# Cross-attention and expert-choice FFN on one core: SBUF tiles placed at 128-byte multiples, three weight units split before the experts begin, gathered quarters turned one by one

## The chip, the cores and the metric

One NeuronCore of a Trainium2 chip runs the whole program. The metric is the device time of one execution in microseconds (us); a "run" is one execution timed from outside, and one execution was also recorded by the hardware profiler. PE is TensorE, DVE VectorE, ACT ScalarE, POOL GpSimd, SP the engine that issues most DMAs.

## The reference, cut to what matters

All in float32, with B=8 batches of S=224 queries, D=512, S2=750 context rows, 16 heads of 32, E=8 experts with I=2048:

```python
Q, K = rope(layernorm(x) @ Wq.T), rope(ctx @ Wk.T)
a = softmax(where(mask == 0, -inf, Q @ K.T / sqrt(32)))
x = x + tanh(g_xattn) * ((a @ (ctx @ Wv.T)) @ Wo.T)
y = layernorm(x)
gating, idx = top_k(transpose(softmax(y @ gate_w.T)), 56)
h = silu(y[idx] @ w_gate[e].T) * (y[idx] @ w_up[e].T)
x = x + tanh(g_ffn) * scatter_add(gating * (h @ w_down[e].T))
```

Each expert takes 56 rows of each batch, 448 rows in all.

## The kernel before, in words

A product that has to be exact to float32 is made of three matmuls in the type float32r: an operand w is split into w_hi (ACT copies it with rounding) and w_lo = w - w_hi (DVE subtracts), and PE adds w_hi x_hi, w_hi x_lo and w_lo x_hi in PSUM. The first operand of a matmul is the stationary one (loaded as weights), the second the moving one, which streams through PE one column at a time.

Three stages follow one another, each a block with barriers at its ends.

- `project_context`: for each batch, keys (L526 to L528, 24 matmuls of 376 moving columns for each of four groups; stationary `w_hi`/`w_lo`, moving `c_hi`/`c_lo`) and values (L537 to L539, 12 matmuls of 512 moving columns for each of six chunks k of 125 context rows; stationary `c_hi`/`c_lo` from row 125k on, moving `w_hi`/`w_lo`). That is 768 and 576 matmuls in the eight batches.
- `attend`: scores (L1282, moving `ks`), masking (L990), exp (L880), transposes (L1298), the product with the values (L1322, moving `e_t`), and between them the remainder of the batch before: projection out (L1222), second layer norm, gate logits, affinity. `every_batch` writes the order of every engine out by hand; `end()` of each engine is what is left after the last batch. There: residual (L1051), `moments` (L964, L967), POOL's `root` (L780, L782), `norm_2` (L975), transposes of xn2 (L1249), two copies into `xT` (ACT L857, DVE L1177), logits (L1262, L1061), affinity (L1063 to L1074), and seven top-8 rounds (L1080 to L1090). POOL's `end()` stores `xn_rows` (L810), adds the NaN flag into `x2o` (L795, two instructions) and stores `out` (L806), then waits for both stores. SP's `end()` loads the first four weight units into `w_raw` (L756), once the last score is made.
- `experts`: each of the 8 experts has 24 weight units of 128 x 1024: 16 for gate and up (`gate_up`, L1622 to L1624, 24 matmuls of 448 columns; moving `xs_hi`/`xs_lo`) and 8 for down (`down`, L1639 to L1641, 24 matmuls of 448 columns; moving `h_hi`, `h_lo`, `h_hi` in turn, one third of them `h_lo`). Units run through a ring of four slots; ACT (L1502) and DVE (L1552) split each unit three ahead (LEAD = 3). That is 3072 matmuls of the first kind and 1536 of the second. Before the first expert, gates and indices are turned onto the slot partitions (L1668), copied into `gate_t` (L1588) and `idx_t` (L1590), POOL copies one expert's indices into `gather_i` (L1469) and starts four indirect DMAs for the quarters of `xg` (L1472), PE turns all four (`turn_rows`, 16 transposes, L1608), and ACT (L1507) and DVE (L1557) split the turned rows into four pairs `xs_hi[:, c]`, `xs_lo[:, c]`. After the last expert there are transposes (L1650), scaling (L1562) and four scatters (L1482).

SBUF tiles are placed one behind another in the order of the code, each rounded up to 32 bytes, the first (`cst`) at byte 16512 of each partition. Worked out from that order, the starts modulo 128 are, before: `w_hi`, `w_lo` 0; `c_hi`, `c_lo` 32, with rows of 3008 bytes, so chunk c starts at 32 or 96 in turn; `ks`, `e_t`, `h_hi`, `ws_hi`, `ws_lo`, `xT`, `qs` 64; `sm`, `wo_sb`, `xs_hi`, `xs_lo`, `h_lo` 0. A key matmul's second half (columns 376 on) starts 1504 bytes later, which is 96 modulo 128; a value's chunk k starts 500k bytes later.

Of the kernel before, what the change touches and what calls it, by code (L numbers as in the profile page):

```python
# [10 lines left out]
U32 = mybir.dt.uint32  # L11
# [31 lines left out]
LEAD = 3  # L43
WAYS = 32
# [25 lines left out]
F_XT, F_Q, F_USES = 0, 2, 4  # L70

# [46 lines left out]
def program(nc, ctxT, x, maskq, wk, wv, wq, wo, gatew, gx, gf, wstream, consts, rotations, out):  # L118
# [5 lines left out]
    with ExitStack() as top:  # L124
# [15 lines left out]
        w_in = [sem(f"w_in{j}") for j in range(NRAW)]  # L140

        with ExitStack() as mid:
# [8 lines left out]
            with ExitStack() as late:  # L151
                sb(late, "below", [P, IC * SLOTS - E_OVER * (KC // 2) * PAIR])
                w_raw = [sb(late, f"w_raw{j}", [P, UNIT]) for j in range(NRAW)]
# [17 lines left out]

            project_context(nc, sem, sb, ps, both, ctxT, wk, wv, wq, x, maskq, gx, gf, consts, rotations, kd, vd, cst, gains)
            attend(nc, sem, sb, ps, both, x, maskq, wo, gatew, kd, vd, xn_rows, out, cst, ident,
                   cos, sin, gains, gate_all, row_all, wstream, w_raw, w_in)
        experts(nc, sem, sb, ps, w_raw, w_in, wstream, xn_rows, out_rows, cst, ident, gains, gate_all, row_all)


def project_context(nc, sem, sb, ps, both, ctxT, wk, wv, wq, x, maskq, gx, gf, consts, rotations, kd, vd, cst, gains):

    with ExitStack() as st:  # L180
        wraw, c_raw, k_split, v_out = both.wraw, both.c_raw, both.k_split, both.v_out
        w_hi = sb(st, "w_hi", [P, 2, DC, D], F32R)
# [422 lines left out]
def attend(nc, sem, sb, ps, both, x, maskq, wo, gatew, kd, vd, xn_rows, out, cst, ident,  # L605
           cos, sin, gains, gate_all, row_all, wstream, w_raw, w_in):

    with ExitStack() as st:
# [8 lines left out]
        sm = sb(st, "sm", [QP, SR, QC, SK])  # L617
        least, sums = sb(st, "least", [QP, KSLOTS, QC]), sb(st, "sums", [QP, 2, QC, HG])
        parts, spread = sb(st, "parts", [QP, 2, QC * HG]), sb(st, "spread", [QP, 2, QC, P])
        e_t = [sb(st, f"e_t{j}", [KP, KC // 2, PAIR]) for j in range(E_OVER, 2 * HG)] + both.e_t  # L620
# [65 lines left out]
        with nc.Block() as block:  # L686
            @block.sync
            def _(sp):
# [164 lines left out]
            def _(act):  # L853
# [95 lines left out]
            def _(dve):  # L949
# [143 lines left out]

                def start():
# [70 lines left out]
                def end():  # L1165
# [232 lines left out]
def experts(nc, sem, sb, ps, w_raw, w_in, wstream, xn_rows, out_rows, cst, ident, gains, gate_all, row_all):  # L1398

    with ExitStack() as st:  # L1400
        h_hi = sb(st, "h_hi", [P, IC, SLOTS], F32R)
        sb(st, "w_raw_place", [P, NRAW, UNIT])
        w_hi = [sb(st, f"ws_hi{j}", [P, UNIT], F32R) for j in range(NRAW)]
        w_lo = [sb(st, f"ws_lo{j}", [P, UNIT], F32R) for j in range(NRAW)]
        gate_t = sb(st, "gate_t", [RP, E, RG])
        idx_t = sb(st, "idx_t", [RP, E, RG], U32)
        gather_i, scatter_i = sb(st, "gather_i", [RP, RG], U32), sb(st, "scatter_i", [RP, RG], U32)
        xg = sb(st, "xg", [RP, RG, D])
        xs_hi, xs_lo = sb(st, "xs_hi", [P, DC, SLOTS], F32R), sb(st, "xs_lo", [P, DC, SLOTS], F32R)
        silu = [sb(st, f"silu{j}", [P, SLOTS]) for j in range(2)]  # L1410
        hid = [sb(st, f"hid{j}", [P, SLOTS]) for j in range(2)]
        h_lo = sb(st, "h_lo", [P, IC, SLOTS], F32R)
        y_cols = sb(st, "y_cols", [P, DC, SLOTS])
        y_sb = sb(st, "y_sb", [RP, RG, D])
# [5 lines left out]
        whi_done, wlo_done = sem("whi_done"), [sem(f"wlo_done{j}") for j in range(NRAW)]  # L1420
# [3 lines left out]
        gathered, x_turned, xhi_done, xlo_done = sem("gathered"), sem("x_turned"), sem("xhi_done"), sem("xlo_done")  # L1424
# [12 lines left out]
        with nc.Block() as block:  # L1437
            @block.sync
            def _(sp):
# [18 lines left out]
            def _(pool):  # L1458
# [5 lines left out]
                def gather(e):  # L1464


                    hold(x_turned, e)
                    hold(gathered, 16 * RG * e)
                    nc.gpsimd.tensor_copy(gather_i[:], idx_t[:, ds(e, 1), :].rearrange("p o g -> p (o g)")).then_inc(gidx_done, 1)  # L1469
                    hold(gidx_done, e + 1)  # L1470
                    for g in range(RG):
                        pool.indirect_dma_start(xg[:, g, :], None, xn_rows, bass.IndirectOffsetOnAxis(gather_i[:, g:g + 1], 0)).then_inc(gathered, 16)  # L1472

                def scatter(e):

                    hold(scattered, 16 * RG * e)
                    nc.gpsimd.tensor_copy(scatter_i[:], idx_t[:, ds(e, 1), :].rearrange("p o g -> p (o g)")).then_inc(sidx_done, 1)
# [7 lines left out]
                pool.wait_ge(idx_ready, 1)  # L1485
# [10 lines left out]
            def _(act):  # L1496
# [39 lines left out]

                for u in range(LEAD):
                    split_w(0, u)
# [199 lines left out]
```

## Time and profile before

| | us |
|---|---|
| median of 3 runs | 1840.67 |
| the three runs | 1840.67, 1841.35, 1837.13 |
| the profiled execution's own time | 1836.25 |
| its span, first to last instruction | 1834.4 |
| PE busy | 1740.8 (95%) |
| DVE / ACT / POOL busy | 1038.9 / 839.2 / 235.4 |

The span is shared out over the stages by the row of each stretch in the view by windows. A row of the timeline gives the start in us, the duration in us, engine, line, operation, tiles (written<-read), shapes and count. Matmul durations overlap, since PE works on several at once: what one costs in a stream is the distance from its start to the next one's start, called its pitch here.

### The profile page before, as it was taken

To read this page: it belongs to the slowest core of one execution; us is meant where nothing else is said; L and a number is where in the kernel's file an instruction comes from. 1 tells how busy PE (TensorE), PEld (TensorE's weight loads), DVE (VectorE), ACT (ScalarE), POOL (GpSimd) and SP (SyncE) were. 2 spreads that over 40 slices of the span, in tenths; PEclk is the share of its full clock that TensorE was granted. 3 is DMA by queue.
4 is the path that set the end of the run, shared out by engine and by line. 5 is a ranking of instruction groups with operands and counts; after the bars stand their busy time and mean duration, and the time that the engine had idled before them with its cause. 6 is when DMAs were issued, how large, how long until landed. Compare 5 with 4: busy or idle time off the path is not lost.

```text
span 1834.4 us, 28481 instructions
## 1 busy us (share of the span) xinstructions
PE 1740.8 (95%) x10502; PEld 1545.1 (84%) x10502; DVE 1038.9 (57%) x1786; ACT 839.2 (46%) x1482; POOL 235.4 (13%) x302
## 2 busy tenths in 40 slices
PE   7999999899999999983999999999999999999995
PEld 6898998677777877753999999999999999999995
DVE  6666667777887787754544535435445354453541
ACT  3223225777776877742433434424344243343430
POOL 0000002131231232122000102002020020010101
PEclk9999999999999999995999999999999999999998
DMA  6544547756755755523333535335343252353421
GB/s 242 224 173 186 189 156 220 182 126 153 178 147 135 183 150 134 141 87 96 115 104 103 150 109 143 103 103 151 106 121 127 106 149 104 101 150 109 124 92 20
DMA packets 76301, 251.90 MB, mean 137 GB/s; under 512 B 10784, under 2 KB 10784, under 8 KB 74928
## 3 DMA queue, kind: packets, MB, share of 16 engines
q1 hardware_dynamic: 64208, 216.55, 38.3%
q0 software_dynamic: 12000, 34.12, 7.9%
q8 instruction: 57, 0.93, 0.2%
q14 instruction: 36, 0.29, 0.1%
HBM read 188.01 MB, written 51.61 MB: 131 GB/s over the span
## 4 chain that ended last, share of the span: by engine, by line
PE 52%; POOL 1%; DVE 0%; issue 0%; DMA 0%; DVEq 0%; ACT 0%; POOLq 0%
PE gu_ps L1624 11%; PE gu_ps L1623 11%; PE gu_ps L1622 11%; PE y_ps L1641 6%; PE y_ps L1640 6%; PE y_ps L1639 6%; PE y_ps L1650 1%; PE gu_ps L1608 1%; POOL out L1482 0%; DMA xg<-xn_rows,gather_i 0%; POOL gather_i L1469 0%; POOL xg L1472 0%; DVE xs_lo L1557 0%; DVE y_cols L1584 0%; PE gu_ps L1668 0%
## 5 line engine op out<-in xcount | busy, mean ns | idle before, releaser
L1622 PE MATMUL gu_ps<-xs_hi,ws_hi 128*128 128x448 f32 x1024 | 370.3, 362 | 3.0 <-DVE xs_lo L1557 3.0
L1624 PE MATMUL gu_ps<-xs_hi,ws_lo 128*128 128x448 f32 x1024 | 371.9, 363 | 0.0
L1623 PE MATMUL gu_ps<-xs_lo,ws_hi 128*128 128x448 f32 x1024 | 371.8, 363 | 0.0
L1552 DVE TENSOR_TENSOR ws_lo<-w_raw,ws_hi 128x1024 fp32r<-128x1024 f32 x192 | 235.2, 1226 | 189.3 <-ACT ws_hi L1502 188.3
L1502 ACT ACTIVATE ws_hi<-w_raw 128x1024 fp32r<-128x1024 f32 x192 | 201.5, 1051 | 163.7 <-PE y_ps L1641 150.6
L1298 PEld LDWEIGHTS t_ps<-cst,sm 112*125 112x125 f32 x1536 | 205.0, 190 | 68.6 <-issue 29.3
L990 DVE CUSTOM_DVE_ANT_0 sm<-m_ps,mq 112x752 f32<-112x752 f32 x256 | 229.7, 935 | 34.2 <-PE m_ps L1282 33.8
L1298 PE MATMUL t_ps<-cst,sm 112*125 112x112 f32 x1536 | 233.3, 281 | 15.0 <-DVE e_t L998 11.3
L880 ACT ACTIVATE sm<-sm,least 112x752 f32<-112x752 f32 x256 | 234.7, 919 | 13.7 <-DVE least L990 12.7
L1622 PEld LDWEIGHTS gu_ps<-xs_hi,ws_hi 128*128 128x128 f32 x1024 | 192.0, 187 | 16.9 <-issue 3.3
L1623 PEld LDWEIGHTS gu_ps<-xs_lo,ws_hi 128*128 128x128 f32 x1024 | 192.7, 188 | 14.6
L1624 PEld LDWEIGHTS gu_ps<-xs_hi,ws_lo 128*128 128x128 f32 x1024 | 192.6, 188 | 10.4
L1523 ACT ACTIVATE silu<-gu_ps 128x448 f32<-128x448 f32 x128 | 69.8, 545 | 274.2 <-PE gu_ps L1624 272.2
L1641 PE MATMUL y_ps<-h_hi,ws_lo 128*128 128x448 f32 x512 | 187.8, 367 | 0.0
L1640 PE MATMUL y_ps<-h_lo,ws_hi 128*128 128x448 f32 x512 | 187.6, 367 | 0.0
L1639 PE MATMUL y_ps<-h_hi,ws_hi 128*128 128x448 f32 x512 | 187.4, 366 | 0.0
L887 ACT ACTIVATE e_t<-t_ps 125x448 f32<-125x448 f32 x256 | 137.4, 543 | 107.6 <-PE t_ps L1298 106.2
L1571 DVE TENSOR_TENSOR hid<-silu,gu_ps 128x448 f32<-128x448 f32 x128 | 79.6, 622 | 188.2 <-ACT silu L1523 188.2
L1482 POOL DMA_INDIRECT out<-y_sb,scatter_i x32 | 52.4, 1637 | 860.5 <-DVE y_sb L1562 853.2
L1574 DVE TENSOR_TENSOR h_lo<-hid,h_hi 128x448 fp32r<-128x448 f32 x128 | 80.0, 625 | 82.5 <-ACT h_hi L1525 81.8
L1282 PE MATMUL m_ps<-ks,qs 96*112 96x376 f32 x512 | 120.0, 355 | 5.0 <-PEq L227 1.7
L1525 ACT ACTIVATE h_hi<-hid 128x448 fp32r<-128x448 f32 x128 | 74.0, 578 | 88.0 <-DVE hid L1571 88.0
(153 smaller groups left out, 2438.6 us busy)
## 6 DMA issues: line engine op xcount, KB each, us to landing
w_raw<-wstream SPq DMA_DIRECT2D x192, 512.0 KB, 3.5
ks<-k_split SPq DMA_DIRECT2D x192, 188.0 KB, 5.4
k_split<-k_split SPq DMA_DIRECT2D x32, 752.0 KB, 3.4
v_rows<-v_out SPq DMA_DIRECT2D x16, 750.0 KB
vs<-v_rows SPq DMA_DIRECT2D x16, 750.0 KB
c_raw<-ctxT SPq DMA_DIRECT2D x7, 1500.0 KB, 13.0
qs<-q_hi POOLq DMA_DIRECT2D x64, 112.0 KB, 5.1
mq_raw<-maskq SPq DMA_DIRECT2D x7, 656.2 KB, 10.9
```

Source lines behind the costliest of these rows:

```text
L880: nc.scalar.activation(rows, rows, ACT.Exp, bias=least[:, h % KSLOTS, qc:qc + 1], scale=-1.0, accum_out=sums[:, h // HG % 2, qc, h % HG:h ...
L887: nc.scalar.activation(e_t[h % (2 * HG)][:, pc], t_ps[tile_of(b, h, pc) % 2][0:KP, 0:PAIR], ACT.Copy).then_inc(t_act, 1)
L990: nc.vector.tensor_tensor_reduce(sm[:, h % SR, qc].rearrange("p (a n) -> p a n", a=2), m_ps[qc][0:QP, :, 0:KN], mq[:, qc].rearrange("p (a ...
L1298: mm = nc.tensor.transpose(t_ps[n % 2][0:KP, a:a + QP], sm[:, h % SR, qc, c * KP:c * KP + KP], ident[0:QP, 0:QP])
L1502: nc.scalar.activation(w_hi[s][:], w_raw[s][:], ACT.Copy).then_inc(whi_done, 1)
L1552: nc.vector.tensor_tensor(w_lo[s][:], w_raw[s][:], w_hi[s][:], ALU.subtract).then_inc(wlo_done[s], 1)
L1622: nc.tensor.matmul(o, w_hi[s][:, w], xs_hi[:, c], start=(c == 0), stop=False)
L1623: nc.tensor.matmul(o, w_hi[s][:, w], xs_lo[:, c], start=False, stop=False)
L1624: mm = nc.tensor.matmul(o, w_lo[s][:, w], xs_hi[:, c], start=False, stop=(c == DC - 1))
L1639: nc.tensor.matmul(o, w_hi[s][:, w], h_hi[:, i], start=(i == 0), stop=False)
L1640: nc.tensor.matmul(o, w_hi[s][:, w], h_lo[:, i], start=False, stop=False)
L1641: mm = nc.tensor.matmul(o, w_lo[s][:, w], h_hi[:, i], start=False, stop=(i == IC - 1))
```

## The change

- Two pads of 64 bytes (`top_edge`, `mid_edge`), another order of the tiles, and rows of 768 instead of 752 elements in `c_hi`/`c_lo`. Worked out as above, all tiles named above now start at 0 modulo 128, and so does every chunk c of `c_hi` and `c_lo` (row 3072 bytes). Not moved to 0: the second half of a key matmul (now 96), a value's chunk k (500k), and the heads of `ks`, whose row stays 3008 bytes (0 or 64 by head, as before but the other way round).
- The tiles `ws_hi` and `ws_lo` exist from the last part of the attention on. ACT splits units 0 to 2 in the attention's `end()`, between `copy_parts` and `x2_columns`; DVE makes their low parts there too: unit 0 after `norm_2`, units 1 and 2 after its copy into `xT`, ahead of the logits.
- For expert 0, DVE writes `gather_i` straight from PSUM, ahead of `gate_t` and `idx_t`; POOL's copy is gone for that expert. SP holds its next weight loads until the four quarters of expert 0 have landed.
- Each quarter has its own semaphore; PE turns a quarter (four transposes) as soon as it has landed. The first unit's matmuls of chunk c wait only for `xs_lo[:, c]`.

```diff
+LINE = 32
+TOP_EDGE, MID_EDGE = 16, 16
+BEFORE = 2 * (B // 2) * D + DC * SLOTS + 2 * SLOTS
+FIRST = BEFORE + 3 * LINE
...
+        sb(top, "top_edge", [P, TOP_EDGE])
...
-                sb(late, "below", [P, IC * SLOTS - E_OVER * (KC // 2) * PAIR])
-                w_raw = [sb(late, f"w_raw{j}", [P, UNIT]) for j in range(NRAW)]
+                sb(late, "below", [P, FIRST - E_OVER * (KC // 2) * PAIR])
+                first = First(
+                    w_raw=[sb(late, f"w_raw{j}", [P, UNIT]) for j in range(NRAW)],
+                    w_hi=[sb(late, f"ws_hi{j}", [P, UNIT], F32R) for j in range(NRAW)],
+                    w_lo=[sb(late, f"ws_lo{j}", [P, UNIT], F32R) for j in range(NRAW)],
...
+            sb(mid, "mid_edge", [P, MID_EDGE])
...
+        c_hi = [sb(st, f"c_hi{j}", [P, DC, SK + LINE // 2], F32R) for j in range(2)]
+        c_lo = [sb(st, f"c_lo{j}", [P, DC, SK + LINE // 2], F32R) for j in range(2)]
...
                     copy_parts(B - 1, NG - 1)
+                    for u in range(LEAD):
+                        act.wait_ge(first.w_in[u], 16)
+                        nc.scalar.activation(first.w_hi[u][:], first.w_raw[u][:], ACT.Copy).then_inc(first.whi_done, 1)
                     x2_columns(B - 1, 0)
...
+                def low_w(u):
+                    dve.wait_ge(first.whi_done, u + 1)
+                    nc.vector.tensor_tensor(first.w_lo[u][:], first.w_raw[u][:], first.w_hi[u][:], ALU.subtract).then_inc(first.wlo_done[u], 1)
...
                     norm_2(b)
+                    low_w(0)
                     dve.wait_ge(rest_made, R_USES * b + R_XNT + 2)
                     nc.vector.tensor_copy(xT[:, 1], m_ps[1][:, 1, 0:2 * S]).then_inc(rest_free, 1)
+                    low_w(1)
+                    low_w(2)
                     logits(b)
...
+                for g in range(RG):
+                    hold(gathered[g], 16)
                 for u in range(NRAW, NU):
                     load(0, u)
...
-                    hold(x_turned, e)
-                    hold(gathered, 16 * RG * e)
-                    nc.gpsimd.tensor_copy(gather_i[:], idx_t[:, ds(e, 1), :].rearrange("p o g -> p (o g)")).then_inc(gidx_done, 1)
-                    hold(gidx_done, e + 1)
+                    if isinstance(e, int) and e == 0:
+                        hold(gidx_done, 1)
+                    else:
...
-                for u in range(LEAD):
-                    split_w(0, u)
                 split_x(0)
...
                 dve.wait_ge(turned, 1)
+                nc.vector.tensor_copy(gather_i, gu_ps[0][0:RP, RG * E:2 * RG * E].rearrange("p (g e) -> p g e", g=RG)[:, :, 0:1]
+                                      .rearrange("p g o -> p (g o)")).then_inc(gidx_done, 1)
...
-                    pe.wait_ge(gathered, 16 * RG * (e + 1))
-                    for c in range(DC):
-                        for g in range(RG):
+                    for g in range(RG):
+                        pe.wait_ge(gathered[g], 16 * (e + 1))
+                        for c in range(DC):
                             mm = nc.tensor.transpose(gu_ps[c][:, g * RP:g * RP + RP], xg[:, g, c * P:c * P + P], ident[0:RP, 0:RP])
...
-                    if u == 0:
-                        pe.wait_ge(xlo_done, DC * (e + 1))
...
                         for c in range(DC):
+                            if u == 0 and k == 0:
+                                pe.wait_ge(xlo_done, DC * e + c + 1)
```

## Rows read from the trace of the kernel before

**Rows 1.** View by windows: us, then busy us (count) per engine, PEclk, DMA
```profile
20.00:215.00 195.00, 195.00 (x984) 175.03 (x983) 130.86 (x175) 57.81 (x84) 0.96 (x2) 1.00 0.51 191
...
860.50:1834.00 973.50, 954.14 (x4848) 889.85 (x4848) 426.62 (x505) 358.67 (x505) 88.35 (x73) 0.99 0.37 114
```

**Rows 2.** Chain of waits, 841 to 861 us: start us, us, what
```profile
841.06 0.94 PE gu_ps L1668 x4
...
842.47 3.36 POOL gather_i L1469
...
846.71 1.05 POOL xg L1472
...
850.55 3.58 DMA xg<-xn_rows,gather_i
...
854.27 3.23 PE gu_ps L1608 x16
...
858.11 2.23 DVE xs_lo L1557 x4
...
860.47 0.71 PE gu_ps L1622
```

**Rows 3.** Timeline, DVE and POOL around the first two gathers
```profile
842.19 0.21 DVE L1590 CAST idx_t<-gu_ps 112x32 uint32<-112x32 f32 x1
842.28 3.48 DVE L1552 TENSOR_TENSOR ws_lo<-w_raw,ws_hi 128x1024 fp32r<-128x1024 f32 x3
...
857.69 0.18 POOL L1469 COPY gather_i<-idx_t 112x4 uint32<-112x4 uint32 x1 [6.21 <-PE gu_ps L1608]
...
858.64 0.95 POOL L1472 DMA_INDIRECT xg<-xn_rows,gather_i  x1 [0.77 <-POOL gather_i L1469]
```

**Rows 4.** Timeline of the attention's end, 809 to 828 us
```profile
809.02 1.86 SPq L756 DMA_DIRECT2D w_raw<-wstream  x4
...
820.71 1.00 DVE L975 TENSOR_SCALAR xn<-x_res,mv,rstd 112x512 f32<-112x512 f32 x2 [1.42 <-POOL rstd L782]
...
823.09 3.11 POOL L795 TENSOR_SCALAR x2o<-x_res,flags_sb 112x512 f32<-112x512 f32 x2
823.17 0.62 DVE L1177 COPY xT<-m_ps 128x448 f32<-128x448 f32 x1 [1.46 <-PE m_ps L1249]
...
827.04 0.17 DVE L1061 COPY lg<-w_ps 112x16 f32<-112x16 f32 x1 [3.25 <-PE w_ps L1262]
```

**Rows 5.** DMA issues (808 to 812 us; whole span): count, KB each, median us to landing
```profile
w_raw<-wstream SPq DMA_DIRECT2D x4, 512.0 KB, 7.2
...
out<-x2o POOLq DMA_DIRECT2D x8, 448.0 KB, 9.5
```

**Rows 6.** Timeline: matmuls of gate and up, 96 starts apart (units 4 to 7 of the second expert)
```profile
1000.44 0.36 PE L1622 MATMUL gu_ps<-xs_hi,ws_hi 128*128 128x448 f32 x1
...
1019.64 0.36 PE L1622 MATMUL gu_ps<-xs_hi,ws_hi 128*128 128x448 f32 x1
```

**Rows 7.** Timeline: matmuls of down, 120 starts apart (the first expert's last five units)
```profile
955.03 0.36 PE L1639 MATMUL y_ps<-h_hi,ws_hi 128*128 128x448 f32 x1
...
979.47 0.37 PE L1622 MATMUL gu_ps<-xs_hi,ws_hi 128*128 128x448 f32 x1
```

**Rows 8.** Timeline: keys (24), values of k=0 (12); then values of k=3 to 5 (36)
```profile
82.63 0.34 PE L526 MATMUL k_ps<-c_hi,w_hi 128*128 128x376 f32 x1
...
86.75 0.39 PE L537 MATMUL v_ps<-w_hi,c_hi 128*125 128x512 f32 x1
...
89.57 0.34 PE L526 MATMUL k_ps<-c_hi,w_hi 128*128 128x376 f32 x1
...
107.55 0.40 PE L537 MATMUL v_ps<-w_hi,c_hi 128*125 128x512 f32 x1
...
115.86 0.34 PE L526 MATMUL k_ps<-c_hi,w_hi 128*128 128x376 f32 x1
```

**Rows 9.** Timeline: ten float32 matmul records of 224 columns, moving `xT`
```profile
506.65 2.06 PE L1208 MATMUL w_ps<-xT,wq_sb 128*128 128x224 f32 x10
```

More of the change, by code:

```diff
@@ L70 @@
 F_XT, F_Q, F_USES = 0, 2, 4
+@dataclass
+class First:
+    w_raw: object
+    w_hi: object
+    w_lo: object
+    w_in: object
+    whi_done: object
+    wlo_done: object
 @dataclass
@@ L605, in attend @@
 def attend(nc, sem, sb, ps, both, x, maskq, wo, gatew, kd, vd, xn_rows, out, cst, ident,
-           cos, sin, gains, gate_all, row_all, wstream, w_raw, w_in):
+           cos, sin, gains, gate_all, row_all, wstream, first):
     with ExitStack() as st:
@@ L617, in attend @@
         sm = sb(st, "sm", [QP, SR, QC, SK])
+        e_t = [sb(st, f"e_t{j}", [KP, KC // 2, PAIR]) for j in range(E_OVER, 2 * HG)] + both.e_t
         least, sums = sb(st, "least", [QP, KSLOTS, QC]), sb(st, "sums", [QP, 2, QC, HG])
         parts, spread = sb(st, "parts", [QP, 2, QC * HG]), sb(st, "spread", [QP, 2, QC, P])
-        e_t = [sb(st, f"e_t{j}", [KP, KC // 2, PAIR]) for j in range(E_OVER, 2 * HG)] + both.e_t
         c_r, cx = sb(st, "c_r", [P, S]), sb(st, "cx", [P, NG, S])
@@ L1395, in _, with experts @@
                 every_batch(start, body, end)
-def experts(nc, sem, sb, ps, w_raw, w_in, wstream, xn_rows, out_rows, cst, ident, gains, gate_all, row_all):
+def experts(nc, sem, sb, ps, first, wstream, xn_rows, out_rows, cst, ident, gains, gate_all, row_all):
     with ExitStack() as st:
[L1401 to L1404, printed above, removed]
+        xg, y_sb = sb(st, "xg", [RP, RG, D]), sb(st, "y_sb", [RP, RG, D])
+        y_cols = sb(st, "y_cols", [P, DC, SLOTS])
+        silu = [sb(st, f"silu{j}", [P, SLOTS]) for j in range(2)]
         gate_t = sb(st, "gate_t", [RP, E, RG])
         idx_t = sb(st, "idx_t", [RP, E, RG], U32)
-        gather_i, scatter_i = sb(st, "gather_i", [RP, RG], U32), sb(st, "scatter_i", [RP, RG], U32)
-        xg = sb(st, "xg", [RP, RG, D])
+        both_i = sb(st, "both_i", [RP, LINE], U32)
+        gather_i, scatter_i = both_i[:, 0:RG], both_i[:, LINE // 2:LINE // 2 + RG]
+        sb(st, "first_place", [P, 3 * NRAW, UNIT])
+        w_raw, w_hi, w_lo = first.w_raw, first.w_hi, first.w_lo
         xs_hi, xs_lo = sb(st, "xs_hi", [P, DC, SLOTS], F32R), sb(st, "xs_lo", [P, DC, SLOTS], F32R)
-        silu = [sb(st, f"silu{j}", [P, SLOTS]) for j in range(2)]
         hid = [sb(st, f"hid{j}", [P, SLOTS]) for j in range(2)]
-        h_lo = sb(st, "h_lo", [P, IC, SLOTS], F32R)
-        y_cols = sb(st, "y_cols", [P, DC, SLOTS])
-        y_sb = sb(st, "y_sb", [RP, RG, D])
+        h_hi, h_lo = sb(st, "h_hi", [P, IC, SLOTS], F32R), sb(st, "h_lo", [P, IC, SLOTS], F32R)
         gu_ps = [ps(st, f"gu_ps{j}", [P, 512]) for j in range(4)]
         y_ps = [ps(st, f"y_ps{j}", [P, 512]) for j in range(RG)]
-        whi_done, wlo_done = sem("whi_done"), [sem(f"wlo_done{j}") for j in range(NRAW)]
+        w_in, whi_done, wlo_done = first.w_in, first.whi_done, first.wlo_done
         w_used = sem("w_used")
```

32 lines of the change are left out of this document (17 added, 15 removed).

## The prediction

> **What bounds the kernel now.** I read the view by windows first, to see which engine a stage waits for. In the projection of the context PE is busy for all 195 us of a 195 us stretch, and from 860.5 us to the end it is busy for 954 of 973 us [rows 1]. So in both stages a matmul's pitch is paid in full, and nothing that DVE, ACT or a DMA gains there counts. The page's 95% for PE hides the rest: between the attention and the experts PE hardly works, and there the chain of waits tells what is paid [rows 2]. It runs from the turning of the indices (PE, 841.06 us) over POOL's copy of them (3.36 us), the start of four gathers, the last one's landing (3.58 us after its issue at 850.55), 16 transposes (3.23 us), ACT's first split, and all four of DVE's, to the first expert matmul at 860.47. The timeline beside it shows why so small a copy takes so long: for the next expert the same copy of 112x4 takes 0.18 us, and here it runs beside DVE's three subtractions of weights, 842.28 to 845.76, and ends with them [rows 3].
>
> Then the pitch. 96 matmuls of gate and up take 19.20 us, 200.0 ns each [rows 6]; 120 of down take 24.44 us, 203.7 each [rows 7], at the same 448 columns. 200.0 ns is (448 + 32) columns at 2.4 GHz. By the layout, what differs is the moving tile: `xs_hi`, `xs_lo`, `h_lo` start at 0 modulo 128 and `h_hi`, which two of down's three matmuls stream, at 64.
>
> **The change part by part.** Its parts add up, as they lie in different stretches.
>
> (1) Indices. The gathers of expert 0 now start after DVE's small copy from PSUM. PE has turned the indices by 842.00 [rows 2]; the like conversion into `idx_t` takes 0.21 us [rows 3], so `gather_i` is there by 842.23. From the end of POOL's copy (845.83) to its first gather are 0.88 us [rows 2], for the next expert 0.77 [rows 3]; I take 0.85 and get 843.08 in place of 846.71, 3.6 us earlier. DVE's and ACT's weight splits leave this stretch altogether; they were on the path only by holding POOL's copy.
>
> (2) Quarters. The fourth issue follows the first by 3.84 us (850.55 - 846.71) and lands 3.58 us after itself: 850.50. That DMA path keeps its price: SP's next weight loads now wait until the quarters are in, which can only help, since before they ran beside the gathers. I leave it at 3.58; the upper bound is the same, the lower one issue distance less, 2.3, as if the quarter before had held it up by all of that. Issues stand 1.28 us apart (3.84/3), four transposes take 0.81 (3.23/4), so only the last quarter's are left when it lands: turned by 850.50 + 0.14 + 0.81 = 851.45, before 857.50. 6.05 us earlier, (1) included.
>
> (3) First matmul. It waits for one part of `xs_lo`, not four. The ACT step and its gaps keep 0.61 us (857.50 to 858.11), one DVE part is 2.23/4 = 0.56, and 0.13 to PE: 852.75 in place of 860.47, **7.7 us** in all. The parts behind it come every 0.56 us, while three matmuls take at least 0.60 [rows 6], so PE does not stall again. SP's held loads of units 4 to 6 are issued near 850.6; of four issued together the median took 7.2 us [rows 5], so the first is in well before 860, and PE wants unit 4 at 852.75 + 4 x 24 x 0.2 = 872 at the earliest. Hidden; if not, the ring of four would stall once.
>
> (4) Low and high parts at the attention's end. ACT waits there for weights that are issued from 809.0 to 810.9 [rows 4] and land 7.2 us later [rows 5], by 818.1. Its three splits, at most 1.16 us each (DVE's 3.48/3 [rows 3]; estimate), are over by 821.6. Behind them queues its copy into `xT`, for which the logits wait; DVE's half of it starts at 823.17 [rows 4], so they end in time. DVE's unit 0 (1.16 us) goes between 821.71 and 823.17, a hole of 1.46 us. Units 1 and 2 (2.32 us) go between 823.79 and 827.04, a hole of 3.25 us [rows 4]. So far the cost is nothing. But POOL adds its flag into `x2o` from 823.09 to 826.20, two instructions of 1.55 us [rows 4], and rows 3 show that a POOL instruction on SBUF and such a DVE subtraction exclude one another. Which of them waits is seen in rows 3 for POOL alone. If POOL waits, it is through at 828.5 in place of 826.20, and the `out` store behind it lands about 10 us later (9.5 in rows 5), by 838.7, before the experts' first instruction at 841.06 [rows 2], which waits for all of the attention: nothing; each us beyond 2.4 would be paid in full. If DVE waits, first for the rest of POOL's first instruction (to 824.65) and then for its second, unit 2 ends at 824.65 + 1.55 + 2.32 = 828.5, 1.5 us after the logits want DVE. I take **-0.5 us**, nearer the case of rows 3, with ends 0 and -1.6. The Trainium skill's page SBUF — State Buffer (Who interferes with whom) says that a DVE instruction with two SBUF inputs and a GpSimd one that reads SBUF share a port pair as a lock, held by whoever starts first. Rows 3 agree for POOL's side (3.35 us for 0.18); by that rule POOL, already running at 823.79, keeps DVE out here, which speaks against this place for units 1 and 2; by it the sum would be 1 us less, 12.6.
>
> (5) Down. `h_hi` moves from 64 to 0. If down then goes as gate and up do, 1536 x 3.67 ns = **5.6 us**. Bounds: 0, and a loss by the second rival.
>
> (6) Projection. Values of k=0 take (89.57 - 86.75)/12 = 235 ns, those of k=3 to 5 (115.86 - 107.55)/36 = 231 [rows 8]; (512 + 32) columns would be 226.7. Their moving tile was at 0 already, so here the stationary one costs. After the change only k=0 starts at 0: 96 x 8.3 ns = **0.8 us**; if every chunk profited, 0.8 + 480 x 4.1 ns = 2.8 us; if none, 0. Keys take (86.75 - 82.63)/24 = 171.7 ns [rows 8], with (376 + 32) columns at 170.0; half of their starts become 0, the other half stay off it. I take 0, with 768 x 1.7 ns = 1.3 us to either side.
>
> (7) The attention's streams. `ks` keeps its mix of offsets: 0. `e_t` goes from 64 to 0, but it is float32, and `xT`, float32 at 64, streams 224 columns in two beats at (2.06 - 0.36)/9 = 189 ns [rows 9], where 448 beats alone are 186.7: nothing to gain. Waits added on PE (three more per `turn_rows`, three in each expert's first unit) and POOL's four more holds per expert stand on things long done in experts 1 to 7: 0.
>
> Sum: 7.7 - 0.5 + 5.6 + 0.8 = **13.6 us**. The profiled execution took 1836.25 us (span 1834.4 and 1.85 around it), so its like would take 1822.6. It is the fastest of the four known; against the median of 1840.67 the sum gives 1827.1, and I forecast **1827**.
>
> **The rivals.**
> A. Placement does nothing. Down changes its PSUM bank every three matmuls, gate and up after twelve, and that could be the 3.7 ns. Against it: values stay twelve in one bank and still lie above their 226.7 [rows 8]. Left is 7.2 us: 1833.5.
> B. Slower. Offsets that are equal disturb one another: in down the moving `h_hi` and the stationary `ws_hi`, `ws_lo` both start at 64, in gate and up 0 meets 64. Then a matmul with equal offsets costs 3.67 x 3/2 = 5.5 ns more, and the change puts every pair of tiles at equal offsets: 3072 of gate and up and 512 with `h_lo`, 3584 x 5.5 = 19.7 us lost, against 7.2 won: 1853. It decides from 2.0 ns per matmul on. For it: keys, whose stationary tile is at 0, have the moving one at 0 in a quarter of them and are 1.7 ns off [rows 8]. Against it: values have moving 0 and stationary tiles at many offsets, none 0, and are worse than keys. The Trainium skill's page TensorE: Matmul & The Clock Gate (Part 2, What happens when you issue a matmul) gives the two operands independent read ports, which would leave B no ground; no row shows that.
> C. All of what a float32r matmul pays beyond its columns goes. Rows 9 show 448 beats in 189 ns. At that pitch 3072 x 11 + 1536 x 14.7 ns = 56 us go, with (1) to (4) 63: 1777. The same page of the Trainium skill (Back-to-back issue gap) has N/2.4 + 2.5 ns for a warm matmul by itself; the estimate from it is 189.2 here. Against it: `xs_hi`, `xs_lo` stream from 0 already and take 200.0.
> D. The hand-over is eaten: A holds, the lock of (4) costs its 1.6, and the gathers land no earlier because their path has a floor that rows 2 do not show; (2) and (3) keep 2.4 + 1.7 of their own. 2.5 us won, 1838.
>
> **How the numbers follow.** Forecast 0.72, A 0.12, B 0.08, C 0.03, D 0.05. A measurement of this kernel tells changes over 0.3% (5.5 us) from none. Faster: forecast, C and most of A, 0.86; same: D and a little of A, 0.06; slower: B, 0.08. Range: the low end is the profiled time less all upper ends, 7.7 + 1.3 (a landing in 2.3) + 5.6 + 2.8 + 1.3 = 18.7: 1817. The high end is A with the 1.6 of (4) and keys at their loss, 1840.67 - 7.7 + 1.6 + 1.3 = 1836. B, C and D, 0.16, are outside.
>
> **What would show it.** Right: no POOL copy before the first gather, which starts near 843; DVE's and ACT's splits of units 0 to 2 before 827; transposes in four groups; first expert matmul 12 us after the indices are turned (852.8 - 841.1), before 19.4; 120 matmuls of down in 24.0 us; 96 of gate and up still in 19.2; k=0 values at 227. Wrong: gate and up above 200.0 (B) or below (C), down at 203.7 (A), logits later than 5.3 us after `norm_2` (4), a wait of PE for `ws_lo` in units 1 to 4 (3).

## The result: 0.47% slower, against a forecast of 0.7% faster

| | before | after |
|---|---|---|
| median of 19 runs each, us | 1839.86 | 1848.73 |
| lowest to highest, us | 1837.13 to 1845.55 | 1842.68 to 1852.75 |
| span of the profiled execution, us | 1834.4 | 1844.1 |
| PE busy, us | 1740.8 | 1760.0 |
| index turning to first expert matmul, us | 841.06 to 860.47 | 840.97 to 853.85 |
| first expert matmul to the start of the last result transpose, us | 955.34 | 971.47 |
| from there to the end, us | 18.6 | 18.8 |

The ratio of the medians is 1.0047, with a 95% interval of 1.0039 to 1.0054: 8.6 us slower (7.2 to 9.9). The profile accounts for its own 9.7 us. The last index instruction of DVE starts at 840.46 us before and at 840.36 after, the first expert matmul comes 6.6 us earlier, the experts lose 16.1, and the tail 0.2.

View by windows of the kernel after, columns as in [rows 1]:

```profile
20.00:215.00 195.00, 195.00 (x981) 174.96 (x980) 130.84 (x174) 57.79 (x84) 0.96 (x2) 1.00 0.52 191
855.00:1844.00 989.00, 969.16 (x4846) 890.04 (x4845) 427.10 (x506) 359.15 (x506) 86.25 (x73) 0.99 0.38 113
```

Each stage still waits for PE alone: 969 us busy in 989, where [rows 1] have 954 in 973.5. DVE and ACT do the same work (427.1 and 359.2 us); PE's grew, and no engine or DMA stands in front of it.

Chain of waits of the kernel after, at the hand-over (start us, us, what), the answer to [rows 2]; `both_i` is the tile that now holds both `gather_i` and `scatter_i`:

```profile
840.97 0.94 PE gu_ps L1701 x4
...
841.93 0.17 DVE both_i L1621
...
842.14 0.85 issue
842.99 1.04 POOL xg L1508
...
845.59 5.07 DMA xg<-xn_rows,both_i
...
850.71 1.77 PE gu_ps L1641 x8
...
852.50 0.55 ACT xs_hi L1542
...
853.08 0.64 DVE xs_lo L1590
...
853.85 0.71 PE gu_ps L1655
```

POOL's copy is gone, and the first gather starts at 842.99, forecast 843.08. PE turns the quarters in groups, and one part of `xs_lo` is enough for the first matmul. One line is off: the chain goes over the third quarter, issued at 845.59 and 5.07 us on its way, not over the fourth with its 3.58 of before. PE's timeline shows it: a group for the first quarter, one for the second, and then eight transposes in a row: the third landed at 850.66, and the fourth, at 851.21, while the third was being turned.

```profile
846.45 0.98 PE L1641 MATMUL gu_ps<-cst,xg 112*128 112x112 f32 x4 [4.56 <-DMA xg<-xn_rows,both_i]
847.70 1.01 PE L1641 MATMUL gu_ps<-cst,xg 112*128 112x112 f32 x4 [0.26 <-DMA xg<-xn_rows,both_i]
850.71 1.76 PE L1641 MATMUL gu_ps<-cst,xg 112*128 112x112 f32 x8 [2.00 <-DMA xg<-xn_rows,both_i]
```

PE's timeline in the experts of the kernel after: 120 starts apart (down, first expert's last five units), 96 apart (gate and up, second expert, units 4 to 7), 96 apart (the same units, third expert):

```profile
950.14 0.36 PE L1672 MATMUL y_ps<-h_hi,ws_hi 128*128 128x448 f32 x1
...
974.46 0.36 PE L1655 MATMUL gu_ps<-xs_hi,ws_hi 128*128 128x448 f32 x1
...
995.85 0.37 PE L1655 MATMUL gu_ps<-xs_hi,ws_hi 128*128 128x448 f32 x1
...
1015.69 0.37 PE L1655 MATMUL gu_ps<-xs_hi,ws_hi 128*128 128x448 f32 x1
...
1117.97 0.37 PE L1655 MATMUL gu_ps<-xs_hi,ws_hi 128*128 128x448 f32 x1
...
1137.43 0.36 PE L1655 MATMUL gu_ps<-xs_hi,ws_hi 128*128 128x448 f32 x1
```

Here is the loss. (974.46 - 950.14)/120 = 202.7 ns for down, against 203.7 in [rows 7]; (1015.69 - 995.85)/96 = 206.7 ns for gate and up, against 200.0 in [rows 6]; (1137.43 - 1117.97)/96 = 202.7 in the next expert. Down follows its expert: its 120 starts from 1071.79 to 1096.59 in the second expert are 206.7 ns apart too. From the third unit of the first expert on, experts 0, 2, 4, 6 run at 202.7 and experts 1, 3, 5, 7 at 206.7, and the pitch changes only where the 16 transposes of a result stand in the stream. The mean is 204.7; before it was (2 x 200.0 + 203.7)/3 = 201.2. So 4608 x 3.4 = 15.8 us are lost. The duration that the profile prints for one matmul (0.36 or 0.37 us) hides this almost wholly: the distance of the starts is the cost.

The spans of two profiled executions also differ by up to some 12 us in the attention's first two batches (122.0 us before, 121.6 after, 121.0 to 133.1 in the experiments, 65.3 for every later batch in all of them); what is said below of times rests on the medians.

### The profile page after: what moved, and what is told of

Read it like the earlier page. It is cut to its first block, busy times and chain, and to the rows that moved or that the text cites. A ratio compares the mean times of both kernels' runs of the same rounds, so it can differ in the third digit from the quotient of the medians.

```text
span 1844.1 us, 28531 instructions
## 1 busy us (share of the span) xinstructions
PE 1760.0 (95%) x10502; PEld 1548.2 (84%) x10502; DVE 1039.3 (56%) x1787; ACT 839.6 (46%) x1482; POOL 230.6 (13%) x301
## 4 chain that ended last, share of the span: by engine, by line
PE 53%; POOL 0%; DMA 0%; issue 0%; DVE 0%; DVEq 0%; ACT 0%; POOLq 0%
PE gu_ps L1655 11%; PE gu_ps L1657 11%; PE gu_ps L1656 11%; PE y_ps L1672 6%; PE y_ps L1673 6%; PE y_ps L1674 6%; PE y_ps L1683 1%; PE gu_ps L1641 1%; POOL out L1518 0%; DMA xg<-xn_rows,both_i 0%; POOL xg L1508 0%; DVE y_cols L1617 0%; PE gu_ps L1701 0%; DVE y_sb L1595 0%; DVEq L1466 0%
## 5 line engine op out<-in xcount | busy, mean ns | idle before, releaser
L1655 PE MATMUL gu_ps<-xs_hi,ws_hi 128*128 128x448 f32 x1024 | 377.0, 368 | 1.4 <-DVE xs_lo L1590 1.4
L1657 PE MATMUL gu_ps<-xs_hi,ws_lo 128*128 128x448 f32 x1024 | 376.2, 367 | 0.0
L1656 PE MATMUL gu_ps<-xs_lo,ws_hi 128*128 128x448 f32 x1024 | 376.1, 367 | 0.0
L1655 PEld LDWEIGHTS gu_ps<-xs_hi,ws_hi 128*128 128x128 f32 x1024 | 192.9, 188 | 18.8 <-issue 1.7
L1518 POOL DMA_INDIRECT out<-y_sb,both_i x32 | 53.2, 1663 | 877.2 <-DVE y_sb L1595 869.9
L1313 PE MATMUL m_ps<-ks,qs 96*112 96x376 f32 x512 | 121.0, 358 | 3.2 <-PEq L247 1.7
```

Source lines behind the costliest of these rows:

```text
L1655: nc.tensor.matmul(o, w_hi[s][:, w], xs_hi[:, c], start=(c == 0), stop=False)
L1656: nc.tensor.matmul(o, w_hi[s][:, w], xs_lo[:, c], start=False, stop=False)
L1657: mm = nc.tensor.matmul(o, w_lo[s][:, w], xs_hi[:, c], start=False, stop=(c == DC - 1))
```

## The experiments

What counts turned out to be the start of a tile modulo 256, not 128. Modulo 256 the kernels stand so, with d = (start of the stationary tile - start of the moving one) modulo 256:

| | `ws` | `xs` | `h_hi` | `h_lo` | d in gate, up | d in down |
|---|---|---|---|---|---|---|
| before | 192 | 0 | 192 | 0 | 192 | 0, 192, 0 |
| after | 128 | 128 | 128 | 128 | 0 | 0 |

**1 to 4: the after kernel with pads.** All four keep the new order of work; only the starts in the experts change. They take these edits, in elements of four bytes, with the kernels that have each in brackets:

```diff
+SPLIT_EDGE = 16      # between w_raw and ws_hi, in attention and experts: ws 192 (1, 2, 4)
+        sb(st, "x_edge", [P, 16])     # before xs_hi (1, 2, 3)
+        sb(st, "hh_edge", [P, 16])    # before h_hi (1)
+        sb(st, "hl_edge", [P, 16])    # before h_lo (1)
```

Starts modulo 256 of `ws`, `xs`, `h_hi`, `h_lo`: the first 192, 0, 64, 128; the second 192, 0, 0, 0; the third 128, 192, 192, 192; the fourth 192 throughout. So d is 192 in gate and up of the first and 128, 64, 128 in its down, 192 everywhere in the second and third, and 0 everywhere in the fourth.

> The changed kernel with only the experts' tiles put back to the old offsets modulo 128: stationary ws_hi/ws_lo at 64, xs_hi/xs_lo at 0, h_hi at 64, h_lo at 0. T1 (what counts is how a matmul's stationary and moving starts lie to one another; equal is dear, 64 apart is free) and T2 (what counts is each tile's own offset, stationary at 0 being dear): gate and up back at 200.0 ns per matmul, down at 203.7, and some 6 to 7 us below the kernel before, 1833, which is what the earlier hand-over is worth. T3 (placement is innocent; the pitch went up by something else in the new schedule, such as the waits per chunk or where the splits run): gate and up stay at 203 to 207, about 1848.

> The changed kernel with the stationary tiles ws_hi/ws_lo alone moved to 64 modulo 128, all moving tiles of the experts left at 0. T1: all 4608 expert matmuls at 200.0 ns, 5.6 us below e1, about 1827. T2: the same 200.0 in gate and up and in down. T3: as the changed kernel, 203 to 207 ns. If down stays at 203.7 with h_hi at 0, its extra came from its bank change (rival A of the prediction).

> The changed kernel with ws_hi/ws_lo left at 0 and all moving tiles of the experts (xs_hi, xs_lo, h_hi, h_lo) at 64. T1: 64 apart again, so 200.0 ns in all, about 1827. T2: stationary at 0 is what is dear, so 203 to 207 ns, about 1848 or above. T3: as the changed kernel.

> The changed kernel with stationary and moving tiles of the experts all at 64 modulo 128. T1: equal offsets, so the 202.7 and 206.7 ns of the changed kernel, about 1848. T2: stationary off 0, so at or near 200.0, with at most what h_hi at 64 cost before, about 1827 to 1833. T3: as the changed kernel.

Measured, beside 21 runs of before (median 1839.26):

| | median, us (runs) | ratio to before, 95% | gate, up, ns | down, ns | start of the last index instruction to first expert matmul, us |
|---|---|---|---|---|---|
| 1, old mix | 1836.19 (11) | 0.9979, 0.9970 to 0.9988 | 200.0 | 204.4 | 12.2 |
| 2, `ws` 192, moving 0, d = 192 | 1830.29 (5) | 0.9948, 0.9934 to 0.9961 | 200.0 | 200.0 | 13.6 |
| 3, `ws` 128, moving 192, d = 192 | 1829.11 (4) | 0.9946, 0.9925 to 0.9966 | 200.0 | 200.0 | 13.5 |
| 4, all at 192, d = 0 | 1842.07 (10) | 1.0009, 0.9996 to 1.0021 | 202.7 | 202.7, in the first expert 206.7 | 13.4 |

PE's timeline in down's last five units of the first expert, 120 starts apart, in the second kernel:

```profile
960.12 0.36 PE L1678 MATMUL y_ps<-h_hi,ws_hi 128*128 128x448 f32 x1
...
984.12 0.36 PE L1661 MATMUL gu_ps<-xs_hi,ws_hi 128*128 128x448 f32 x1
```

The same in the fourth:

```profile
955.41 0.37 PE L1677 MATMUL y_ps<-h_hi,ws_hi 128*128 128x448 f32 x1
...
980.21 0.37 PE L1660 MATMUL gu_ps<-xs_hi,ws_hi 128*128 128x448 f32 x1
```

24.00 us against 24.80 for the same 120 matmuls on the same data. The fourth has the two pitches of after at other absolute starts, so neither 0 nor 64 modulo 128 is a bad place in itself; against the fourth the second shifts the moving tiles alone and the third the stationary ones alone, and both reach 200.0 everywhere. It is the pair that counts. The stretch shown of the fourth is its dear one: 206.7 holds for 8 of its 192 units, from the 16 transposes of gathered rows in the first expert (at 948.9 us) to the transposes of that expert's result, and all else runs at 202.7. That is why it stands at 1842 and not at the 1848 that was expected. And the new hand-over by itself wins: the first kernel is 3.9 us faster than before although its down is 1536 x 0.8 = 1.2 us dearer. Its expectation, 1833 us and 203.7 ns in down, was off because its starts repeat those of before modulo 128 only.

**5: a scan of starts.** A kernel of matmuls alone; it leaves out the whole reference and copies x to the output. Bursts of 48 float32r matmuls with a stationary load each, twelve to a bank as in gate and up, with 1, 4 and 3 transposes ahead of the bursts:

```python
nc.tensor.matmul(u_ps[k][:, 0:n], wt[:, s // 4 + (q // 3 % 8) * P:s // 4 + (q // 3 % 8) * P + P],
                 mt[:, m // 4 + c * 448:m // 4 + c * 448 + n], start=(q % 12 == 0), stop=(q % 12 == 11))
```

> A kernel of matmuls alone: float32r, 128x128 stationary and 448 moving columns (some pairs 376 or 512), three bursts of 48 for each pair of starts (stationary s, moving m, in bytes modulo 256), one to four float32 transposes between bursts. It computes nothing of the reference; x is copied to the output. T1: the pitch follows (s - m) modulo 128 alone: 200.0 ns at 64, 202.7 or 206.7 at 0 whatever m is, s = 128 or 192 like 0 or 64, and 32 and 96 somewhere between. T2 (own offsets): (0,64) and (64,64) differ from what T1 says. If 32 and 96 also give 200.0, only equal starts collide. 376 columns: 170.0 at 64 apart and 172 to 174 at equal starts. 512: 226.7 at 64 apart and up to 235 at 0.

With (s, m) the two starts and 448 columns it gave 202.7 ns at (0, 0), 202.2 at (64, 0), 203.8 at (128, 0) and 200.0 at (192, 0), 200.0 at (0, 64), but 202.2 at (128, 64), and 206.7 at (64, 64). So (64, 0) and (192, 0), the same modulo 128, are not the same: the rule in its form modulo 128, in which 64 apart was free either way, fell. A difference of 192 modulo 256, the stationary start 64 bytes below the moving one, is what was free each time; (32, 96) is the third such pair.

**6: before with `h_hi` and `h_lo` exchanged.** `h_lo`, one third of down, now starts at 192 and `h_hi`, two thirds, at 0; nothing else of before is touched.

```diff
-        h_hi = sb(st, "h_hi", [P, IC, SLOTS], F32R)
+        h_lo = sb(st, "h_lo", [P, IC, SLOTS], F32R)
...
-        h_lo = sb(st, "h_lo", [P, IC, SLOTS], F32R)
+        h_hi = sb(st, "h_hi", [P, IC, SLOTS], F32R)
```

> The kernel before with the places of h_hi and h_lo exchanged: h_hi, streamed by two of down's three matmuls, now starts at 0 modulo 128 and h_lo at 64, where ws_hi and ws_lo start. T1: the equal starts fall from two in three to one in three, so down goes from 203.7 to about 201.8 ns, 2.8 us in all, 1836.5, gate and up stay at 200.0. Rival A of the prediction (down's bank change): down stays at 203.7 and the time at 1839.3.

1837.54 us (10 runs) against 1839.44 (19), ratio 0.9986, 0.9977 to 0.9996. The same 120 starts as in [rows 7]:

```profile
955.04 0.37 PE L1639 MATMUL y_ps<-h_hi,ws_hi 128*128 128x448 f32 x1
...
979.30 0.37 PE L1622 MATMUL gu_ps<-xs_hi,ws_hi 128*128 128x448 f32 x1
```

202.2 ns, where [rows 7] give 203.7, with the same change of bank every three matmuls. The expectation had 201.8 ns. 202.2 is (2 x 200.0 + 206.7)/3, one third at the disturbed pitch of 206.7; but the same sum does not give the 203.7 of before (204.5 with two thirds at 206.7, 201.8 with two thirds at 202.7), nor do the scan's pitches give the 204.4 of kernel 1 (203.3). In a stream that mixes distances the pitches of unmixed streams don't add up, and no scan mixed them. The prediction's rival A, placement does nothing, falls.

**7: the second kernel with the three splits back at the experts' start.** ACT's and DVE's splits of units 0 to 2 leave the attention's end; the rest is kernel 2.

```diff
-                    for u in range(LEAD):
-                        act.wait_ge(first.w_in[u], 16)
-                        nc.scalar.activation(first.w_hi[u][:], first.w_raw[u][:], ACT.Copy).then_inc(first.whi_done, 1)
...
-                    low_w(0)
...
-                    low_w(1)
-                    low_w(2)
...
+                for u in range(LEAD):
+                    split_w(0, u)
```

> e2 with the splits of units 0 to 2 put back where they were, at the experts' start; DVE still writes gather_i from PSUM first, and the quarters are still turned as they land. If POOL's copy was all that the splits held up, the first expert matmul still comes 13.4 us after the last index is made (20.0 before), within 0.5, and the time is e2's, 1830. If DVE's subtractions also hold up POOL while it issues gathers, the first gather or its followers come up to 3.4 us later, so about 16.5 us and 1833.

POOL's timeline of this kernel at the gathers:

```profile
847.14 3.67 POOL L1508 DMA_INDIRECT xg<-xn_rows,both_i  x1 [15.24 <-DVE both_i L1623]
851.12 0.95 POOL L1508 DMA_INDIRECT xg<-xn_rows,both_i  x1 [0.30 <-issue]
852.37 0.93 POOL L1508 DMA_INDIRECT xg<-xn_rows,both_i  x1 [0.30 <-issue]
```

DVE's timeline beside it:

```profile
846.41 3.49 DVE L1587 TENSOR_TENSOR ws_lo<-w_raw,ws_hi 128x1024 fp32r<-128x1024 f32 x3
```

The first gather's issue, 1.04 us in the kernel after, takes 3.67 and is over 0.91 us after DVE's three subtractions; the others take their usual 0.95. ACT's three splits beside it run from 845.10 to 848.05 and end 2.8 us before that issue does, so they are not what it waits for. So it is not only a POOL copy that such subtractions hold: they hold the issue of an indirect DMA too. The first expert matmul comes 15.9 us after the start of the last index instruction, 13.6 in kernel 2. The median, 1830.15 us (10 runs, ratio 0.9950, 0.9935 to 0.9964), does not tell these 2.3 us from nothing: the interval is +-2.7 us wide.

**8: the scan again, modulo 256, with one to six transposes ahead of each burst of 36.** The edit is the list of starts and lengths and `enumerate((1, 2, 3, 4, 5, 6))`; it too leaves out the reference and copies x to the output.

> The kernel of matmuls alone again, six bursts of 36 for each pair of starts, after one to six transposes. R1: for 448 columns (s - m) modulo 256 decides, and 192 alone is free: (192,0), (64,128), (128,192) at 200.0 ns in every burst; (192,128), (0,192) differ by 64 and stand at 202.2; (0,0) and (64,64) change between 202.7 and 206.7 with the number of transposes before the burst, since both states hold once entered. R2: modulo 128 as first thought, then (192,128) and (0,192) are at 200.0 too. 512 columns: e5 had 226.7 at equal starts and 230 to 233 at 20 to 116; if the rule moves with the length, another difference than 192 is free, and (64,64), (128,128) are as (0,0). 376: one free difference near 192 at 170.4, the others 172 to 174.

PE's timeline of this kernel, one row a burst of 36 matmuls; the first two have both starts at 0, the next four both at 64, the last two have 192 and 0:

```profile
34.11 7.54 PE L69 MATMUL u_ps<-mt,wt 128*128 128x448 f32 x36
...
41.85 7.55 PE L69 MATMUL u_ps<-mt,wt 128*128 128x448 f32 x36
...
65.06 7.67 PE L69 MATMUL u_ps<-mt,wt 128*128 128x448 f32 x36
...
72.70 7.54 PE L69 MATMUL u_ps<-mt,wt 128*128 128x448 f32 x36
...
80.32 7.67 PE L69 MATMUL u_ps<-mt,wt 128*128 128x448 f32 x36
...
88.19 7.55 PE L69 MATMUL u_ps<-mt,wt 128*128 128x448 f32 x36
...
111.52 7.46 PE L69 MATMUL u_ps<-mt,wt 128*128 128x448 f32 x36
...
118.95 7.45 PE L69 MATMUL u_ps<-mt,wt 128*128 128x448 f32 x36
```

A burst is 35 pitches and 0.45 us for its two ends: 7.54 is a pitch of 202.7, 7.67 one of 206.7, 7.46 one of 200.0. With both starts at 64 the two alternate from burst to burst; with both at 0, against the expectation, every burst from the second on has 202.7. So the stream falls into one of two patterns and keeps it. The experts of the kernel after do the same, with 16 transposes between them. What picks the pattern is not shown: the number of transposes grows with each burst here, so it can't be told from the mere order, and in scan 5, with 1, 4 and 3 of them, (64, 64) stood at 206.7 all three times. All pairs of scans 5 and 8 with starts at multiples of 32, by d:

| d | 448 columns, ns | 512 columns | 376 columns |
|---|---|---|---|
| 0 | 202.7 or 206.7 | 226.7 to 227.9 | 173.3 |
| 32 | 204.4, once 203.3 | 233.3 | 173.3 |
| 64 | 202.2 | 233.3 | 170.0 to 173.3 |
| 96 | 200.0 or 206.7 | 234.4 | 171.7 |
| 128 | 203.8 | 232.6 to 233.3 | 173.3 |
| 160 | 205.3 | 233.3 | 173.3 |
| 192 | 200.0 (five pairs, every burst) | 228.9 | 170.4 |
| 224 | 200.0 to 206.7 | 233.3 | 173.3 |

The lowest value of each column is the column count + 32 at 2.4 GHz: 200.0, 226.7, 170.0. Which d gives it goes by the length: 192 for 448, 0 for 512. At 448 columns 192 gave 200.0 in every burst; it was expected to be the only one, but 96 gave it too, in seven bursts of nine. 376 columns reach 170.0 in one burst only, at 64; 384 columns reach their 173.3 at 192 in every burst and at 0 in two of six. Starts off this grid of 32 don't fit the table: (16, 16) has 200.3, (80, 16) has 206.7 and (0, 16) 200.0. So the distance alone is the rule only for starts at multiples of 32, as all tiles of the experts have them.

**9: the third kernel with `c_hi` and `c_lo` moved too**, for the projection's sake (their start goes from 128 to 192, that of `w_hi`, `w_lo` is 128):

```diff
+        sb(st, "c_edge", [P, LINE // 2])
         c_hi = [sb(st, f"c_hi{j}", [P, DC, SK + LINE // 2], F32R) for j in range(2)]
```

> e3 (stationary weights at 128 modulo 256, moving tiles of the experts at 192) with c_hi and c_lo also moved by 64: in the first half of the keys the stationary w_hi is then at 128 and the moving c_hi at 192, the difference of e3. R1: those 384 matmuls go from 173.3 to 170.4 ns, 1.1 us; values change by what their own table gives (between -2 and +2 us); the experts stay at 200.0. Time as e3 within 2 us, 1828.

1828.12 us (5 runs) against 1839.00 (15), ratio 0.9935, 0.9921 to 0.9950: the fastest of all, 12.0 us below before by its ratio, though its interval overlaps that of kernel 3. Keys of the first half go from 173.1 to 170.4 ns, those of the second from 173.2 to 172.1, and values stand at 232.7 to 234.8.

**10: kernel 2 with `x_edge` at 48 elements instead of 16**, so the moving tiles start at 128 modulo 256. That is 64 bytes apart as in kernel 2, but the other way round: d = 64.

```diff
-        sb(st, "x_edge", [P, 16])
+        sb(st, "x_edge", [P, 48])
```

> e2 with the experts' moving tiles 128 bytes further on: stationary at 192 modulo 256, moving at 128, so still at 64 and 0 modulo 128. R1 (modulo 256): the difference is now 64 and not 192, so 202.2 ns in all 4608 matmuls, 10 us above e2, 1840. R2 (modulo 128): 200.0 ns and e2's time, 1830.

Gate and up of the second expert, 96 starts apart:

```profile
993.87 0.37 PE L1661 MATMUL gu_ps<-xs_hi,ws_hi 128*128 128x448 f32 x1
...
1013.29 0.37 PE L1661 MATMUL gu_ps<-xs_hi,ws_hi 128*128 128x448 f32 x1
```

202.3 ns, and 24.26 us for down's 120, 202.2: the scan's value for d = 64, in all of the experts. 1838.75 us (10 runs), ratio 0.9994, 0.9982 to 1.0007. So a scan of bare matmuls gave beforehand what the placement costs in the full kernel, sign included.

**All of it together.** Let the hand-over win 5.9 us (6.6, less 0.7 below) and take each kernel's pitches from its own timeline:

| | hand-over | experts, us | sum against before | measured, 95% |
|---|---|---|---|---|
| after | -5.9 | 4608 x 3.4 = +15.8 | +9.9 | +8.6, 7.2 to 9.9 |
| 1 | -5.9 | 1536 x 0.8 = +1.2 | -4.7 | -3.9, -5.5 to -2.2 |
| 2 | -5.9 | -1536 x 3.7 = -5.6 | -11.5 | -9.6, -12.1 to -7.2 |
| 3 | -5.9 | -1536 x 3.7 = -5.6 | -11.5 | -9.9, -13.8 to -6.3 |
| 4 | -5.9 | 4608 x 1.6 = +7.4 | +1.5 | +1.7, -0.7 to +3.9 |
| 6 | 0 | -1536 x 1.5 = -2.3 | -2.3 | -2.6, -4.2 to -0.7 |
| 7 | -5.9 + 2.3 | -5.6 | -9.2 | -9.2, -12.0 to -6.6 |
| 9 | -5.9 | -1536 x 3.7 = -5.6 | -11.5 | -12.0, -14.5 to -9.2 |
| 10 | -5.9 | 3072 x 2.2 - 1536 x 1.5 = +4.5 | -1.4 | -1.1, -3.3 to +1.3 |

Measured is what the ratio makes of the median of before. Every sum lies in its interval, that of after at its very edge, and nothing is fitted: the hand-over is that of the kernel after throughout (with 2.3 more in kernel 7), the pitches are each kernel's own, and the projection is left out. The hand-over that kernel 1's one profile shows is 1.3 us shorter than that of after; taken into the sum it would make it -6.0, just outside. (For kernel 4: 202.7 in 184 units and 206.7 in 8 is a mean of 202.8, before 201.2.)

## Why the prediction was wrong, step by step

(1) **Indices: right.** First gather at 842.99, forecast 843.08; DVE's copy takes 0.17 us for 0.21.

(2) **Quarters: 1.1 us too early.** The last turning was forecast to end at 851.45 and ended at 852.47. The transposes' time held; the landing did not. 15 of the third quarter's 16 parts were in by 848.77, the last at 850.66, and the fourth quarter landed 4.38 us after its issue. Kernels 2, 3, 4, 7 and 9 show a like delay: their third quarter takes 4.9 to 5.2 us from its issue. Kernel 1 had none, 3.3 us, and so 12.2 us from the start of the last index instruction to the first matmul, which is the forecast's 852.75 - 840.5. I had kept 3.58 us as the price of the DMA path, from one profile. The cause is not shown, but one thing goes with it. In all the late profiles one packet of 16 KB of an instruction queue starts 2.0 to 3.0 us after the issue of the third gather, while the quarters move (in the kernel after at 847.8 us, for 1.5 us); in kernel 1 it came 0.6 us before the first gather's issue, and in before after the last landing; in kernel 10, 3.2 us after the issue, the third quarter takes 3.6 us and the fourth 4.3.

(3) **First matmul: right, behind (2).** 853.85 in place of 852.75; ACT's and DVE's steps take 0.55 and 0.64 us. PE is not held in the units behind it. One thing was left out: PE had been busy for only 3.75 us of the 11.8 before it, and the first 12 matmuls start 0.373 us apart, up to 858.5 (the level of 1.2 GHz, granted clock 0.50, then 0.98); in the kernel before it was the first 8. Four more at 0.173 us extra are 0.7 us given back.

(4) **Low and high parts at the attention's end: costs nothing, forecast 0.5.** DVE's timeline of the kernel after, 821 to 828 us:

```profile
821.54 1.22 DVE L1120 TENSOR_TENSOR ws_lo<-w_raw,ws_hi 128x1024 fp32r<-128x1024 f32 x1
...
823.08 0.62 DVE L1206 COPY xT<-m_ps 128x448 f32<-128x448 f32 x1 [0.32 <-PE m_ps L1280]
823.62 2.35 DVE L1120 TENSOR_TENSOR ws_lo<-w_raw,ws_hi 128x1024 fp32r<-128x1024 f32 x2
826.95 0.17 DVE L1084 COPY lg<-w_ps 112x16 f32<-112x16 f32 x1 [0.98 <-PE w_ps L1293]
```

POOL's of the same stretch:

```profile
823.00 4.32 POOL L815 TENSOR_SCALAR x2o<-x_res,flags_sb 112x512 f32<-112x512 f32 x2
```

The copy of the logits starts at 826.95, in [rows 4] at 827.04: DVE's three parts fit into its holes to the full. POOL waited, 4.32 us for 3.11, the end that I had put at nothing. By the rule of the Trainium skill that I weighed there (SBUF — State Buffer, Who interferes with whom: the lock goes to whoever starts first), DVE should have waited, since POOL's instruction was under way from 823.00. It did not: its two parts took 1.18 us each, as in [rows 3]. Nor did the first of POOL's two instructions wait: it takes 1.58 us in both kernels, with one of DVE's parts beside it from 823.62 on, and only the second, which starts at 824.57, is stretched, from 1.55 to 2.75 us. No row shown here has DVE waiting for POOL.

(5) **Down: here the prediction failed.** The step read "`h_hi` moves from 64 to 0. If down then goes as gate and up do", and took it for granted that gate and up stay at 200.0. It described a matmul by where its moving tile starts. The runs show that in an unmixed stream with starts at multiples of 32 it goes by the distance from the stationary tile's start to the moving one's, modulo 256, and by the length. Gate and up, which the sum had at no change, went from 200.0 to 202.7 and 206.7 ns, and down from 203.7 to the same two, 15.8 us lost in all where 5.6 were to be won. Gate and up were fast before not because `xs` began at a round address but because `ws` began 64 bytes short of the next multiple of 256. The change moved both to 128 and took the good pair from 3072 matmuls and from the third of down that had it. The rows could not say so by themselves: of the two pairings at 448 columns, (192, 0) and (192, 192), both readings fit.

(6) **Projection: near nothing, forecast 0.8 won.** PE's timeline of the kernel after, 24 keys and 12 values of k=0:

```profile
82.12 0.34 PE L546 MATMUL k_ps<-c_hi,w_hi 128*128 128x376 f32 x1
...
86.28 0.40 PE L557 MATMUL v_ps<-w_hi,c_hi 128*125 128x512 f32 x1
...
89.08 0.33 PE L546 MATMUL k_ps<-c_hi,w_hi 128*128 128x376 f32 x1
```

The values take (89.08 - 86.28)/12 = 233.3 ns, not 227, and the keys (86.28 - 82.12)/24 = 173.3 where [rows 8] have 171.7; the stage ends 0.4 us later than before (the last value matmul starts at 288.96, before 288.59). Keys went to the bad side of my +-1.3. Values keep a riddle: k=0 has d = 0 after the change, for which the scan has 226.7 at 512 columns; but its stationary tile has 125 columns, the scan's 128. That was not tried.

(7) **The attention's streams: right.** From the third on, every batch takes the same time, and the last index is ready within 0.1 us of before.

**The rivals.** B came true in kind, and nearly in size. "Equal offsets disturb one another" was derived from the same rows, priced at 19.7 us lost and 1853 us; 15.8 were lost and the median is 1848.73. Its 5.5 ns a matmul lies between the two patterns that equal starts showed, 2.7 and 6.7. The nearness is partly luck: 5.5 was taken out of a mixed stream by a sum that experiment 6 and kernel 1 don't bear out, and B too reckoned modulo 128. I gave it 0.08, and wrote against it that values, with no equal offsets, are worse than keys, and quoted the Trainium skill's page TensorE: Matmul & The Clock Gate (Part 2, What happens when you issue a matmul), by which independent read ports leave B no ground. Both were poor reasons. Values have another length, and by the scan another good distance (0, not 192), and the page speaks of a structure without saying what a pitch depends on; the runs decide against what I drew from it. A falls by kernel 6, and by kernels 2 and 3, where down has its bank change and 200.0 ns. C falls: no row of any kernel shows 448 columns in under 200.0. D falls: the hand-over was not eaten.

What stays open is why: which part of PE or of the SBUF makes two reads at this distance fit, why the good distance depends on the length, and what picks between 202.7 and 206.7. The runs show the rule, not its cause.

## What to carry to other kernels

Read a matmul's cost as the distance of starts over a hundred of them, and take the starts of both its operands as one setting: moving all to one round address made the expert matmuls 3.4 ns dearer in the mean here, while a pad of 64 bytes at one place was worth some 18 us. A scan of bare matmuls at the kernel's own column count gives the good distance before any layout is changed, and a term of a prediction that rests on one fitted variable should be priced under the other one too. Where DVE works with two SBUF inputs, keep POOL's copies and its DMA issues out of that time.

## What was not expected of the hardware

- Float32r matmuls of 448 columns with a stationary load each: 200.0 ns at a distance of 192 bytes modulo 256, 202.2 at 64, 203.8 at 128, 202.7 or 206.7 at 0, for starts at multiples of 32. For 512 columns 0 is the good distance (226.7 to 227.9), and most others give about 233.
- With equal starts the stream holds one of two pitches for a whole expert (over 500 matmuls), and changes from one to the other only where transposes stand in it; what picks is open.
- A subtraction on DVE with two SBUF inputs stretched the issue of an indirect DMA on POOL from 1.04 to 3.67 us, and took its usual 3.5 us for three itself.
- The two first batches of the attention vary by some 12 us between executions of kernels that don't differ there, with PE idle for up to 5.5 us at a time (kernel 7); every later batch takes 65.3 us.
